# Graph kernel, building stage: one list tile of five scaled on ScalarE instead of two, four on VectorE instead of three

## The reference, cut to what matters

```
h = relu(layernorm(x));  x = x + hypergraph_conv2(relu(hypergraph_conv1(h)))     # segment sums over the edges, four hops
h = relu(layernorm(x))
e = silu(silu([h[src], h[dst], w] @ eW1 + eb1) @ eW2 + eb2)                      # one row for each edge
agg = segment_sum(e, src);  x = x + silu([h, agg] @ nW1 + nb1) @ nW2 + nb2
```

## Time and profile before

| what | value |
|---|---|
| runs, us | 8292.96, 8347.98, 8357.12; median 8347.98 |
| profiled execution, us | 8329.03, of which the span is 8327.0 |
| building stage, about | 148 to 3050 us of the span |
| granted TensorE clock, mean | 0.960 |
| PE, DVE, ACT, POOL busy, share of the span | 91%, 85%, 63%, 38% |

### The profile page before, as it was taken

One profiled execution on the slowest core, in us unless ns is written; L12 is line 12 of the kernel. 1 busy time (PEld: TensorE's weight loads), 2 busy tenths in 40 slices (PEclk: granted clock), 3 DMA queues, 4 the chain that ended last, 5 costly groups with the idle time before them and its releaser, 6 DMA issues. The chain is left out here.

```text
span 8327.0 us, 251689 instructions
## 1 busy us (share of the span) xinstructions
PE 7609.5 (91%) x80310; PEld 7121.8 (86%) x80310; DVE 7068.4 (85%) x15142; ACT 5286.8 (63%) x12950; POOL 3205.9 (38%) x4182
## 2 busy tenths in 40 slices
PE   1999999999999979999788899958999999999996
PEld 1888888888888879999788888858999999999994
DVE  7999999999999967775898888648999999999993
ACT  2899899898999940000677788625666666666662
POOL 4999999999999930000000000001111111111110
PEclk9999999999999989998999999859999999999998
DMA  2778777777777786664899999644333434333432
GB/s 68 160 175 173 170 175 171 173 173 168 177 171 173 173 194 190 191 190 122 197 222 223 216 245 246 164 126 129 116 116 115 116 114 117 113 117 113 116 115 70
DMA packets 1523000, 1309.63 MB, mean 157 GB/s; under 512 B 797344, under 2 KB 1337364, under 8 KB 1521212
## 3 DMA queue, kind: packets, MB, share of 16 engines
q1 hardware_dynamic: 1506126, 1269.86, 62.5%
q0 software_dynamic: 14112, 26.84, 1.2%
q10 hardware_dynamic: 1840, 0.53, 0.0%
HBM read 777.89 MB, written 361.62 MB: 137 GB/s over the span
## 5 line engine op out<-in xcount | busy, mean ns | idle before, releaser
L675 POOL TENSOR_SCALAR OH<-iot,kd 128x102 bf16<-128x102 bf16 x3440 | 2624.1, 781 | 0.0
L2270 POOL DMA_INDIRECT Qx<-tab_q,tidx x294 | 354.3, 1205 | 4680.5 <-DVE skt L2304 2582.3
L980 ACT ACTIVATE RB<-PS 128x512 uint8<-128x512 f32 x2401 | 1409.1, 601 | 117.8 <-PE PS L840 83.5
L1491 PE MATMUL wp<-AF,XS 128*128 128x256 f32 x9604 | 1194.6, 283 | 166.2 <-issue 130.8
L856 PE MATMUL HP<-T3a,RB 128*128 128x193 bf16 x9604 | 1213.3, 250 | 128.9 <-ACT RB L980 128.7
L1491 PEld LDWEIGHTS wp<-AF,XS 128*128 128x128 f32 x9604 | 1146.1, 190 | 197.6 <-issue 197.4
L1517 ACT ACTIVATE AF<-RG 128x1536 fp32r<-128x1536 uint8 x686 | 1022.6, 1491 | 329.1 <-PE wp L1491 216.9
L2291 ACT ACTIVATE Z<-Zb 128x512 f32<-128x512 f32 x882 | 556.0, 630 | 977.5 <-DVE Zb L2348 977.5
L856 PEld LDWEIGHTS HP<-T3a,RB 128*128 128x128 fp8e4 x9604 | 867.3, 98 | 215.4 <-issue 157.7
L2241 PEld LDWEIGHTS p<-eW2s,Y 128*128 128x128 f32 x7056 | 923.8, 191 | 23.9
L1571 DVE CAST AF<-RG 128x2048 fp32r<-128x2048 uint8 x686 | 811.9, 1222 | 143.4 <-DMA RG<-adjT 49.7
(11 more groups left out here) (340 smaller groups left out, 15054.1 us busy)
## 6 DMA issues: line engine op xcount, KB each, us to landing
RG<-adjT SPq DMA_DIRECT2D x1372, 224.0 KB, 6.7
sdb<-bk SPq DMA_DIRECT2D x245, 768.0 KB
adj<-RB SPq DMA_DIRECT2D x343, 448.0 KB, 2.9
adjT<-RT SPq DMA_DIRECT2D x686, 224.0 KB, 3.7
RG<-adj SPq DMA_DIRECT2D x686, 224.0 KB, 4.6
sdb<-bk SPq DMA_DIRECT2D x49, 384.0 KB
WR<-wk SPq DMA_DIRECT2D x882, 9.0 KB
tab_p<-Pst SPq DMA_DIRECT2D x25, 512.0 KB, 3.0
```

The costliest lines, as they stand in the source:

```text
L675: ins = e.tensor_scalar(OH[:, g * GT + k, :], iot1[:, 0:KEYS], kd[:, g * GT + k:g * GT + k + 1], None, ALU.is_equal)
L980: e.activation(RB[n % NSLOT][:, k, :].bitcast(u8).rearrange("p (n x) -> p n x", x=2), bank(u)[:, :].rearrange("p (x n) -> p n x", x=2), AC ...
L1491: ins = e.matmul(ps[b][:, 0:256], lhsT=XS[:, n * PB + m, :, :].rearrange("p c f -> p (c f)"), rhs=AF[:, (b + n) % 3, m, :], start=n == 0 a ...
```

## The change

`AT` goes from 2 to 1. In every group ACT scales one tile of `LB` and no longer two (two instructions fewer), and DVE's `tensor_tensor` writes four tiles instead of three.

```
--- before.py
+++ after.py
@@ -21,7 +21,7 @@
 TC = 70
 CAP = TC * P
 GT = 5
-AT = 2
+AT = 1
 TWO = 2.0 ** -9
 NGR = TC // GT
 KEYS = 102
```

## The result

The changed kernel takes 8409.52 us (median of 9 runs, 8363.44 to 8434.5) against 8347.98 us before: a ratio of 1.0077, 95% interval 1.0052 to 1.0101. It is slower, by 62 us between these medians (65 against 8344.27, the median of nine runs of the kernel before), inside the range and inside the 1% that I called no change. The forecast was 8372, so the growth was forecast at about half its size.

The account below looks back on a forecast made before the run. POOL was taken to bound the building stage, DVE close behind. DVE's 58.63 us and POOL's 58.55, plus 0.1, gave a 58.7 us turn, 0.7 more in some 48 turns: +34 us on 8338.5, forecast 8372 us, range 8325 to 8440.

Parts of the forecast that it names:

- no change within 1%: Whole kernel: the measured time stays within 1% of the kernel before; chance 0.76.
- the 58.5 to 58.9 us that were forecast: Building stage, line 660: the length of a turn the profile after would show, 58.02 us before.
- the first rival: Line 1063 against line 675: DVE's larger multiply shuts POOL out; turn 59.72 us, 8427 us; 0.22, shared with the steep slope.
- POOL bounds the turn, with DVE close behind: Building stage: POOL, 99.0% busy, waits for no other engine and sets the 58.02 us turn; DVE is 95.5% busy.
- ACT's relief is worth only the 0.40 us ahead of `cb`: Head of the turn: two fewer scalings bring `cb` 0.40 us earlier; DVE's wait at line 1034 shrinks from 1.12 to 0.64.
- The larger multiply costs 1.04 ns an element, 1.70 us a turn: DVE's `LH`, line 1063: one more tile, 1632 elements a turn, 1.70 us; range 1.04 to 1.79 ns an element.
- DVE's turn of 58.63 us: DVE's turn without its wait for POOL: 58.02 - 0.61 + 1.70 - 0.48 = 58.63 us.
- POOL's turn grows by 0.31 us for each us of DVE, 0.53 us in all: POOL's one-hots: mean loss beside all DVE work, 1.70 x 0.31 = 0.53 us; POOL's turn 58.55, bounds 58.02 and 59.72.
- The forecast of 58.7: Building stage: DVE's 58.63 us and POOL's 58.55 meet, plus 0.1 for unevenness; a turn 0.7 us longer.
- The rival in which `LH` shuts POOL out: Same as the first rival: each us of `LH` costs POOL a full us, 1.70 us a turn, +88 us.
- its sign in the profile: Line 1047 still waits 0.6 us a turn or more and the turn is over 59.5 us: POOL was shut out.
- the one-hot of 1.24 us: POOL's one-hot said to begin beside line 1112's `OA` and end beside line 1114's `OD`; evidence for POOL being shut out.

Follow-up runs that it names:

- e10: Kernel before, with POOL's three larger diagonal instructions (2.4 us a turn) left out: turn 56.78 us, ratio 0.9929 to the kernel before.
- e13: Kernel before, with the diagonal made by ACT at the head of group 2 instead of by POOL: 8274.33 us against 8330.07, ratio 0.9923.
- e8: Kernel before, with ACT scaling three tiles and DVE two in the widest groups (6 of 14): turn 57.42 us, ratio 0.9980.
- e2: Changed kernel, but ACT still makes the second tile's scalings, into scratch nobody reads: turn 59.74 us, ratio 1.0074 to the kernel before.
- e11: Changed kernel, with POOL's three larger diagonal instructions left out: turn 58.24 us, 8344.33 us, ratio 1.0004 to the kernel before.
- e6: Kernel before, plus a DVE scratch memset of 2 w + 50 columns behind every three-tile multiply: turn 59.72 us, ratio 1.0097.
- e7: Kernel before, plus a DVE product of two fp32 SBUF tensors (w / 2 + 30 columns) behind every three-tile multiply: turn 59.75 us, ratio 1.0066.
- e1: Changed kernel, with DVE's four-tile multiply cut into two instructions of two tiles each: turn 60.54 us, ratio 1.0128 to the kernel before.
- e9: Kernel before, with DVE's third unit of a group moved from ahead of line 1056 to behind it: turn 59.77 us, ratio 1.0086.
- e4: Kernel before, with ACT leaving out the second tile's two scalings and DVE still doing three tiles: turn 58.53 us, ratio 1.0017.
- e12: Kernel before, with ACT scaling one tile in group 0, three in groups 4, 5, 6, 11 and 12, two elsewhere: turn 57.65 us, ratio 0.9964.
- e3: Kernel before, without ACT's second-tile scaling, with a DVE scratch memset (2 w columns) before its three-tile multiply: turn 58.51 us, ratio 1.0007.

## Why the prediction was right, and where not

The forecast of no change within 1% and the range came out. The mechanism did so in part, and the time owes something to luck: the turn of 59.76 us lies outside the 58.5 to 58.9 us that were forecast, and the growth of a turn was 1.74 us, not 0.68. The measured time is inside the range since the range was stretched to 8440 us for the first rival, whose turn is the one that came.

*POOL bounds the turn, with DVE close behind.* Right as far as POOL's work counts: taking 2.4 and 2.75 us of it from POOL and nothing from DVE's program shortened the turn by 1.24 and 1.48 us (e10, e13). But POOL's pace isn't its own. In e8 and e10 DVE hardly waits for POOL and POOL not at all for DVE, and yet they keep in step (POOL is 2.2 to 6.8 us ahead at group 3 from turn 5 on in e10).

*ACT's relief is worth only the 0.40 us ahead of `cb`.* Right in size (the wait went from 1.12 to 0.65 us, forecast 0.64). It paid nothing, though: e2, without the relief, has the same turn, and DVE waits that much less for POOL.

*The larger multiply costs 1.04 ns an element, 1.70 us a turn.* Right: 1.03 ns. DVE's busy time grew from 55.4 to 57.0 us. Its lower bound was misread: between 144 and 288 elements give (466 - 353) / 144 = 0.78 ns, less than the 1.04 called the smallest.

*DVE's turn of 58.63 us.* A little high. e11 shows DVE's lead at 58.24, and e10 shows 56.78 for the kernel before, where my way of working it out (the turn less the wait for POOL) gives 57.41. The visible wait of 0.61 us is half of what went when POOL was relieved. The other half is DVE's own busy time, which fell from 55.4 to 54.8 us with the same program: this suggests that DVE's instructions are held up beside POOL's too (`SP` of line 1047 takes 271 ns before and 258 in e10, line 1114 708 and 700). The growth of 1.46 us from e10 to e11 is 1.9 of DVE's busy time less 0.50 in front of `cb`.

*POOL's turn grows by 0.31 us for each us of DVE, 0.53 us in all.* This term failed. POOL's turn grew by 1.74 us, as much as the multiply adds to DVE. I had divided POOL's whole loss by DVE's whole work, as if the loss were a share of DVE's time that any further time would pay alike. It isn't spread like that, as the counts below show: only some of DVE's instructions cost POOL anything. But dividing by these alone doesn't save the term. They take some 38 us of a turn (each counted up to the start of the next instruction), so 17.7 / 38 = 0.47 us for each us and 0.79 us for the larger multiply (an estimate), still less than half of what came. The term had made the two engines meet at 58.6; in fact the turn is 59.76, with DVE waiting 0.95 us in it for POOL. The forecast of 58.7 lacks 1.06 us a turn, 52 us over 49 turns.

*The rival in which `LH` shuts POOL out.* It had this very number, 59.72 us, and its sign in the profile (line 1047 still waiting, a turn over 59.5) is what came. Its reason is right in kind: the larger multiply is one of the instructions beside which POOL loses time. As the whole account of this growth it isn't shown, since the memset of e6 cost as much as the product of e7, and cutting the multiply in two (e1) did not help. The Trainium skill, SBUF — State Buffer, section "Who interferes with whom", says that a DVE instruction with two SBUF inputs contends with a GpSimd instruction that reads SBUF, and that one with at most one such input, outside the 2-port modes, does not. The one-hots of the kernel before agree with the first half, as the counts below show. On the second half no run decides: POOL's turn grew with memsets that read nothing, but each of these stands directly behind line 1063, which reads two.

*Which of DVE's instructions hold POOL.* This the trace of the kernel before answers, from 300 to 2900 us, if each one-hot is set against the DVE instructions that run beside it, each of these counted up to the start of the next. Of 3137 one-hots, 468 lie beside none of lines 1056, 1063, 1112 and 1114 (which read two tensors in SBUF each): they take 527 to 625 ns, 533 on average. The 571 that touch line 1036, which reads one tensor in PSUM and one in SBUF, take at most 547. The 1491 that touch line 1114 take 636 at least and 986 on average, the 1007 that touch line 1063 816 on average. So the whole loss, (786 - 533) x 70 = 17.7 us a turn, is met beside these four lines. The prediction's example shows it too, if read with care: the one-hot of 1.24 us doesn't end beside the `OD` of line 1114 but at 1518.86, 0.34 us behind its end, and so lies beside all of it. In e6 the 488 one-hots beside none of these lines and no memset still take 533 ns; the others became longer.

*What takes its place.* Shown: POOL's one-hots have no fixed length. They last 0.52 us beside an idle DVE and 786 ns before; 801 to 814 with the larger multiply or with an instruction behind it (e1, e2, e6, e7), and 811 where DVE only works in another order (e9). Seen too: a held one-hot ends at a nearly fixed distance behind the start of a DVE instruction. DVE and POOL of the changed kernel, where DVE comes to the end of turn 25 and POOL makes the one-hots of turn 26:

```profile
1690.30 0.95 DVE L1063 TENSOR_TENSOR LH<-LB,pl 128x704 f32<-128x704 bf16 x1
1691.17 0.41 DVE L1112 TENSOR_TENSOR OA<-iot,SBs 128x512 bf16<-128x512 bf16 x1
1691.50 0.75 DVE L1114 TENSOR_TENSOR OD<-iot,SBd 128x1024 bf16<-128x1024 bf16 x1
```

```profile
1689.65 1.04 POOL L675 TENSOR_SCALAR OH<-iot,kd 128x102 bf16<-128x102 bf16 x1
...
1690.67 1.23 POOL L675 TENSOR_SCALAR OH<-iot,kd 128x102 bf16<-128x102 bf16 x1
```

The first one-hot ends at 1690.69, 0.39 us behind the start of the multiply; the second at 1691.90, 0.40 us behind the start of the large one-hot of line 1114. In the kernel before, 903 one-hots from 300 to 2900 us take over 0.9 us, and 656 of them end 0.36 to 0.44 us behind the start of a DVE instruction. A one-hot beside the long instructions gets done when DVE goes on to its next one. Argued from this: POOL advances by so many one-hots for so many of DVE's instructions, so DVE time that is added between them, read or not, is added to POOL's turn too. This fits e6, e7 and the change, the lockstep of e8, and e9 in so far as the order matters. It does not by itself give the size in e9, where DVE's busy time fell, nor explain e4, nor e1, where one more end in each group should have served POOL. Why a memset costs POOL as much as a product stays open.

## What to carry to other kernels

When two engines slow each other, the price of more work on one of them is not their mean loss so far: allow for the whole of the added time, and not even that is a bound (e9 added none, and the turn grew by 1.75 us). Count the slower instructions by what ran beside them before taking a mean over everything. A wait that the profile shows (0.61 us) says who is late, not by how much the other engine could go faster; taking work from the late one (e10, e13) does. And of four engines above 90%, look for the one that waits for nobody and that others wait for; the first half alone is true of POOL in e10 as well. Two small multiplies and two copies moved from POOL to ACT gained 0.8%, where shifting tiles between DVE and ACT moved waits about and gained 0.2% (e8, not clear of no change) and 0.4% (e12).

## What was not expected of the hardware

- Fourteen memsets a turn on DVE that read nothing (140 to 247 ns each, e6) went with POOL's one-hots growing from 786 to 803 ns, as much as with products of two tensors (e7).
- No one-hot on POOL beside DVE's line 1114 took under 636 ns; those beside none of its four long two-input lines took 533 ns on average.
- In e8 POOL and DVE kept in step for over 35 turns (4.1 or 4.6 us apart at group 3), neither waiting for the other.
- Another order of DVE's instructions alone took POOL's one-hots from 786 to 811 ns, and the turn up by 1.75 us (e9).
- Two ACTIVATEs fewer in each group (e4) made the turn 0.5 us longer in the profile, not shorter; the time (1.0017) isn't clear of no change.
- A memset of 48 to 176 columns between an instruction and the one that waits for its result cost DVE no busy time (55.6 us a turn in e3 with it, in e4 without).
